# One-hot matrices made by three wide comparisons per group, with the weighing split between two engines

## The chip, the cores and the metric

The kernel runs on one core of a Trainium2 chip. The metric is device time in microseconds (us): the median of three runs of the kernel before is 2552.06 us (2551.03 to 2554.61). Where the text speaks of engines, PE is TensorE (matrix products; PEld are its weight loads), DVE is VectorE, ACT is ScalarE, POOL is GpSimd and SP is SyncE, which here only issues transfers.

## The reference

A graph of 3125 nodes and 103125 edges (both directions of 50000 random pairs, and a loop at each node, sorted by target) is used in two layers. The first makes ten hops of a normalised sum over neighbours, the second four steps of a gated unit whose messages depend on the edge's type.

```python
agg = jax.ops.segment_sum(feat[src] * e[:, None], dst, num_segments=N_NODES)   # first layer, 10 times
...
m = (embedding @ W_msg.T + b_msg).reshape(n, N_EDGE_TYPES, DIM)
q = m[src, etype]
r = jax.ops.segment_sum(q, dst, num_segments=n)                                # second layer, 4 times
embedding = _gru_cell(r, embedding, w_ih, w_hh, b_ih, b_hh)
```

Every sum over edges is a product with a matrix of counts: how many edges of each type go from node s to node t. The kernel builds this matrix once, on the chip, and uses it in all fourteen sums.

## The kernel before, in words

**Stages.** First the edges are loaded and turned into tables (`keys`, `tab`), 125 edges to a column, 825 columns. Then comes the counting stage, from 63.5 us to 534.1 us, in which all that the diff touches happens. After it come a check of the degrees, ten hops, and four steps of the gated unit.

**The counting stage.** The targets are cut into 125 groups of 25 nodes. The edges of one group lie in at most W = 8 columns of the tables (with a rare extra column, which an `If` on a loaded number handles). For a group q:

- POOL copies the eight columns' keys, weights and places into small buffers (`stage`, lines 361 to 366), and waits before that for the buffer to be free.
- DVE makes two one-hot matrices (`onehots`, lines 959 to 968). `hot_place` marks for each edge which of 128 places its source has: one comparison of 1024 elements. `hot_pair` marks for each edge which of 228 pairs (target within the group, source within its tile) it belongs to, multiplied by the edge's weight, a power of two that encodes its type: eight instructions of 228 elements, one a column.
- PE multiplies the two, column by column, eight products summed in one bank of PSUM (`count`, lines 599 to 612). Each product waits for its own `hot_pair` instruction (`s_hot`).
- ACT copies the sum from PSUM to `words` (`evacuate`, lines 457 to 461).

Eight groups are a block. After a block ACT cuts the three bytes (lanes) of its words apart (`part_lanes`, line 471, three instructions), SP stores them, and DVE sums the packed digits (`sum_digits`, lines 983 to 995, six instructions). All four engines run loops whose bodies are written out: on DVE 16 groups and two digit sums a turn, seven turns. The one-hot buffers are double, so POOL, DVE and PE are at most two groups apart.

Order on each engine is the order of the program; engines wait for each other by semaphores only. `wait_ge` stands in front of the instruction that follows it.

## Time and profile before

| | |
|---|---|
| median of three runs | 2552.06 us |
| profiled execution | 2550.86 us, its span 2549.3 us |
| counting stage (63.5 to 534.1 us) | 470.6 us of the span |
| PE busy | 2190.8 us, 86% |
| DVE busy | 1488.7 us, 58% |
| ACT busy | 335.0 us, 13% |
| POOL busy | 134.9 us, 5% |

The shares are means over stages with different limits. The rows below are of the counting stage, apart from one of the stage behind it that stands for a form of instruction.

### The profile page before, as it was taken

How to read it: one execution, taken by the hardware profiler on the slowest of the kernel's cores; microseconds unless marked ns; L12 is line 12 of the kernel's file. 1: busy time of each engine (PE TensorE's matmuls, PEld its weight loads, DVE VectorE, ACT ScalarE, POOL GpSimd, SP SyncE). 2: the span in 40 equal slices, each digit the busy share in tenths (PEclk: the TensorE clock that was granted, in tenths of full speed). 3: DMA queues.
4: the chain of work that ended last, by engine and by line, in shares of the span. 5: the costliest groups of instructions: out<-in, count | busy, mean ns of one | idle time of the engine just before them, and what ended most of it. 6: DMA issues, size and time to landing. Idle time of an engine off the chain costs nothing.

```text
span 2549.3 us, 41289 instructions
## 1 busy us (share of the span) xinstructions
PE 2190.8 (86%) x14375; PEld 1440.7 (57%) x14886; DVE 1488.7 (58%) x3473; ACT 335.0 (13%) x494; POOL 134.9 (5%) x391
## 2 busy tenths in 40 slices
PE   1544545559999999999799999999999999999996
PEld 1322333348999898988644455444554446544464
DVE  6988999977777777777662234522444324442243
ACT  0322223330000000000121011210112100220000
POOL 1322222200000000000000000000000000000000
PEclk9996555559999999999899999999999999999998
DMA  2000000010000000001400000000000000000001
GB/s 72 21 21 21 21 21 21 28 41 2 1 2 2 2 2 2 1 2 49 139 1 1 1 1 1 1 1 1 1 1 1 1 1 1 1 1 1 1 1 50
DMA packets 22188, 34.32 MB, mean 13 GB/s; under 512 B 2450, under 2 KB 18442, under 8 KB 21469
## 3 DMA queue, kind: packets, MB, share of 16 engines
q1 hardware_dynamic: 19025, 30.56, 3.5%
q8 instruction: 127, 2.08, 0.3%
q10 hardware_dynamic: 2944, 0.93, 0.2%
q14 instruction: 92, 0.75, 0.1%
HBM read 18.04 MB, written 13.45 MB: 12 GB/s over the span
## 4 chain that ended last, share of the span: by engine, by line
PE 75%; DVE 15%; issue 5%; DVEq 2%; DMA 2%; ACT 0%; POOLq 0%; ACTq 0%; POOL 0%
PE ps L787 41%; PE ps L706 26%; DVE hot_pair L967 8%; PE ps L739 3%; PE ps L727 2%; DVEq L961 2%; DVE dig L990 1%; DVE hot_place L964 1%; DVE big L993 1%; DMA big<-in_L_gnn_w_hh 1%; PE ps L647 1%; DMA x_after_hops<-x 1%; PE ps L691 1%; PE ps L605 1%; DVE dig L992 1%
## 5 line engine op out<-in xcount | busy, mean ns | idle before, releaser
L787 PE MATMUL ps<-slots,m_parts 125*128 125x500 fp8e4 (+1 forms) x5600 | 1088.0, 354 | 6.6 <-DVE m_parts L1337 5.2
L787 PEld LDWEIGHTS ps<-slots,m_parts 125*128 125x128 f16 x5600 | 547.4, 98 | 495.7 <-issue 10.0
L706 PE MATMUL ps<-parts,big 125*128 125x256 f16 x6125 | 669.6, 273 | 6.8 <-issue 4.2
L706 PEld LDWEIGHTS ps<-parts,big 125*128 125x128 fp8e4 x6125 | 591.3, 98 | 63.6
L605 PE MATMUL ps<-hot_pair,hot_place 125*128 125x228 f16 x1000 | 230.6, 400 | 256.5 <-DVE hot_pair L967 256.5
L1255 DVE TENSOR_SCALAR slots<-big 128x3200 int32<-128x3200 int32 (+1 forms) x112 | 244.1, 2183 | 279.8 <-PE ps L787 279.7
L605 PEld LDWEIGHTS ps<-hot_pair,hot_place 125*128 125x128 f16 x1000 | 143.1, 149 | 343.8 <-DVE hot_pair L967 283.1
L967 DVE TENSOR_SCALAR hot_pair<-iota_pair,win 125x228 f16<-125x228 f16 x1000 | 262.5, 334 | 3.1 <-issue 3.1
L1357 DVE SCALAR_TENSOR_TENSOR r_parts<-ps,over,r_parts 128x500 f16<-128x500 f32 (+1 forms) x28 | 19.1, 684 | 230.1 <-ACT r_parts L527 230.1
L1364 DVE SCALAR_TENSOR_TENSOR gate_r<-ps,over,gate_r 128x500 f32<-128x500 f32 (+1 forms) x28 | 19.1, 682 | 229.3 <-PE ps L739 221.8
L1183 DVE SCALAR_TENSOR_TENSOR hop_tmp<-ps,coef,g 125x128 f32<-125x128 f32 x250 | 87.6, 350 | 97.9 <-PE ps L706 94.4
L461 ACT ACTIVATE words<-ps 128x228 int32<-128x228 f32 x125 | 72.0, 602 | 354.4 <-PE ps L605 352.2
L964 DVE TENSOR_TENSOR hot_place<-iota_place,win_p 125x1024 f16<-125x1024 f16 x125 | 85.5, 684 | 48.2 <-issue 32.1
L727 PE MATMUL ps<-w_parts,emb_parts 128*125 128x512 f16 x300 | 84.7, 397 | 17.7 <-DVE m_full L1343 9.3
L527 ACT ACTIVATE r_parts<-ps,over 128x500 f16<-128x500 f32 (+1 forms) x28 | 17.7, 634 | 618.6 <-PE ps L787 618.6
L427 ACT ACTIVATE rs<-rs 125x25 f32<-125x25 f32 x3 | 0.7, 224 | 708.7 <-DVE rs L852 708.7
L1185 DVE SCALAR_TENSOR_TENSOR hop_tmp<-ps,coef,hop_tmp 125x128 f32<-125x128 f32 x250 | 87.8, 351 | 8.9
L1164 DVE TENSOR_SCALAR parts<-hop_tmp,scale 125x128 f16<-125x128 f32 x225 | 64.3, 286 | 36.4 <-DVE hop_tmp L1185 33.0
L1178 DVE SCALAR_TENSOR_TENSOR g<-hd,anchor,hop_tmp 125x128 f32<-125x128 f32 x225 | 79.0, 351 | 9.4 <-DVE hop_tmp L1177 0.7
L1167 DVE SCALAR_TENSOR_TENSOR parts<-hop_tmp,scale,parts 125x128 f16<-125x128 f32 x225 | 79.1, 352 | 8.0
L364 POOL TENSOR_TENSOR win<-keys,q_off 125x8 f32 (+1 forms) x125 | 65.3, 523 | 332.7 <-DVE hot_pair L967 318.5
L1343 DVE SCALAR_TENSOR_TENSOR m_full<-ps,bias_msg 125x512 f32<-125x512 f32 x100 | 68.3, 689 | 24.6 <-PE ps L727 23.6
(200 smaller groups left out, 1130.2 us busy)
## 6 DMA issues: line engine op xcount, KB each, us to landing
packed_counts<-packed SPq DMA_DIRECT2D x16, 625.0 KB, 3.3
big<-packed_counts SPq DMA_DIRECT2D x4, 1600.0 KB, 7.3
big<-packed_counts SPq DMA_DIRECT2D x3, 1200.0 KB, 6.5
hd<-in_x SPq DMA_DIRECT2D x1, 1562.5 KB
x_again<-in_x SPq DMA_DIRECT2D x1, 1562.5 KB
x_after_hops<-x SPq DMA_DIRECT2D x1, 1562.5 KB
big<-x_after_hops SPq DMA_DIRECT2D x1, 1562.5 KB
out<-big SPq DMA_DIRECT2D x4, 250.0 KB
```

The lines of the kernel that those rows point to most:

```text
L605: pe.matmul(ps[:, j, 0:KP], hot_place[0:CH, b, :, w], hot_pair[0:CH, b, w, :], start=w == 0, stop=w == W - 1, skip_group_check=True).then_ ...
L706: last = pe.matmul(ps[:, n % RING, 0:2 * F], tot_f8[0:Q, c, a, :], both((parts0, parts1)[par], a), start=a == 0, stop=a == TILES - 1)
L727: last = pe.matmul(ps[0:Q, 6 + a % 2, :], emb_parts[:, h, a, :], w_parts[:, w, :], start=n == 0, stop=n == 2)
L739: last = pe.matmul(out, g_parts[:, w, j * F:(j + 1) * F], value(h), start=start and m == 0, stop=stop and m == 2)
L787: last = pe.matmul(ps[:, k % 2, 0:SIZES[k] * Q], m_parts[0:Q, a, h, t * F:(t + 1) * F], slots_f8[0:Q, t % 2, 0:SIZES[k], a, 0:Q], start=a ...
L964: TT(hot_place[0:CH, b, :, :], iota_place[0:CH, :, :], win_p[0:CH, b:b + 1, :].broadcast_to([CH, 128, W]), ALU.is_equal)
L967: TS(hot_pair[0:CH, b, w, :], iota_pair[0:CH, :], win[0:CH, b, 0, w:w + 1], win[0:CH, b, 1, w:w + 1], ALU.is_equal, ALU.mult).then_inc(s_h ...
L1167: return STT(out=at[:, 1, :], in0=value, scalar=power, in1=at[:, 0, :], op0=ALU.mult, op1=ALU.subtract)
L1178: step(STT(out=tile_of(g, c), in0=tile_of(hd, c), scalar=anchor[0:Q, ds(h, 1)], in1=hop_tmp[0:Q, 2, :], op0=ALU.mult, op1=ALU.add))
L1183: step(STT(out=hop_tmp[0:Q, 0, :], in0=bank[:, 0:F], scalar=column(coef, c), in1=tile_of(g, c), op0=ALU.mult, op1=ALU.add))
L1185: step(STT(out=hop_tmp[0:Q, 1, :], in0=bank[:, F:2 * F], scalar=column(coef, c), in1=hop_tmp[0:Q, 0, :], op0=ALU.mult, op1=ALU.add))
L1255: TS(slots[:, t % 2, 0:n * 4].bitcast(I32).rearrange("p (n b w) -> p n b w", b=NB, w=2), big1[:, first:first + n * 4].bitcast(I32).rearran ...
```

## The change

For each group DVE now issues three instructions in place of nine. `marks` compares all eight columns with 128 places in one instruction (1024 elements, laid out column by column and no longer interleaved). `hot_pair` compares all eight columns with the 228 pairs in one instruction (1824 elements), without the weight. The weight now goes into the other factor, `weighed = marks * weight`: for the first WA = 5 columns ACT does this, one instruction of 128 elements a column with the weight as a scale, and for the last WD = 3 columns DVE does it in one instruction (384 elements). In the comparisons the small operand is read through a pattern whose innermost run is two elements: POOL writes each key, place and weight twice, side by side, and the pattern reads that pair 64 or 114 times before it goes on to the next column.

Around that: buffers are four deep (DEPTH) and no longer two; POOL does four small instructions a group and no longer three; PE waits once for the pairs, five times for ACT's columns and once for DVE's; ACT's `evacuate` of a group comes after the weighing of the group two later, and the three lanes of a block are cut apart one at a time, after the fourth, fifth and sixth group of the next block; `sum_digits` has five instructions and no longer six, and stands after the seventh group of the next block; the loops of DVE and ACT have 32 groups written out (three turns), that of PE 16. Key spacing KQ goes from 1024 to 456, and the differences are now held in 16 bits; a path for inputs that need larger counts is adapted and doesn't run with these inputs.

```diff
+DEPTH = 4
+ROUND = 4
+WA = 5
+WD = W - WA
...
+            def stage_window(q, b):
+                lo = pool.value_load(windows[0:1, ds(q, 1)], min_val=0, max_val=NCH)
+                pool.wait_ge(s_hot_used, q + 1)
...
+                pool.tensor_copy(win_place[0:CH, b, :, :], twice(tab[0:CH, 0, ds(lo, W)]))
+                pool.tensor_copy(win_f[0:CH, b, :, :], twice(tab[0:CH, 1, ds(lo, W)]))
+                pool.tensor_copy(win_w[0:CH, b, :], tab[0:CH, 1, ds(lo, W)])
+                pool.tensor_tensor(win_key[0:CH, b, :, :], twice(keys[0:CH, ds(lo, W)]),
+                                   q_off[0:CH, ds(q, 1)].rearrange("p (w o) -> p w o", o=1).broadcast_to([CH, W, 2]),
+                                   ALU.subtract).then_inc(s_wst, 1)
...
+            def weigh(q, b):
+                act.wait_ge(s_marks, q + 1)
+                for w in range(WA):
+                    act.activation(weighed[0:CH, b, w, :], marks[0:CH, b, w, :], ACT.Copy,
+                                   scale=win_w[0:CH, b, w:w + 1]).then_inc(s_weighed, 1)
+
+            def block_of(turn, b, n, turn_before):
                 blk = 2 * turn + b
-                act.wait_ge(s_bytes, blk + 1)
                 for j in range(n):
-                    evacuate(blk, b, j)
-                part_lanes(blk, turn, b, BQ * blk + n - 1)
...
+                    weigh(BQ * blk + j, j % DEPTH)
+                    if j >= 2:
+                        evacuate(blk, b, j - 2)
+                    elif turn_before is not None:
+                        evacuate(2 * turn_before + 1 - b, 1 - b, BQ - 2 + j)
+                    if 3 <= j < 3 + LANES and turn_before is not None:
+                        part_lane(turn_before, 1 - b, j - 3, 16 * turn_before + BQ * (1 - b) + BQ - 1)
...
                 pe.wait_ge(s_taken, q + 1)
+                pe.wait_ge(s_pairs, q + 1)
                 for w in range(W):
-                    pe.wait_ge(s_hot, W * q + w + 2 * W + 1)
-                    pe.matmul(ps[:, j, 0:KP], hot_place[0:CH, b, :, w], hot_pair[0:CH, b, w, :],
-                              start=w == 0, stop=w == W - 1, skip_group_check=True).then_inc(s_hot_used, 1)
+                    if w < WA:
+                        pe.wait_ge(s_weighed, WA * q + w + 1)
+                    elif w == WA:
+                        pe.wait_ge(s_weighed_d, q + 1)
+                    last = pe.matmul(ps[:, j, 0:KP], weighed[0:CH, b, w, :], hot_pair[0:CH, b, w, :],
+                                     start=w == 0, stop=w == W - 1, skip_group_check=True)
+                last.then_inc(s_hot_used, 1)
...
-                dve.wait_ge(s_hot_used, W * q + W)
-                TT(hot_place[0:CH, b, :, :], iota_place[0:CH, :, :],
-                   win_p[0:CH, b:b + 1, :].broadcast_to([CH, 128, W]), ALU.is_equal)
-                for w in range(W):
-                    TS(hot_pair[0:CH, b, w, :], iota_pair[0:CH, :], win[0:CH, b, 0, w:w + 1],
-                       win[0:CH, b, 1, w:w + 1], ALU.is_equal, ALU.mult).then_inc(s_hot, 1)
+                dve.wait_ge(s_hot_used, q + 1)
...
+                def row(m, count, n):
+                    return m.rearrange("p (o n two) -> p o n two", o=1, two=2).broadcast_to([CH, count, n // 2, 2])
+
+                def each(m, count, n):
+                    return m.rearrange("p w (o two) -> p w o two", o=1).broadcast_to([CH, count, n // 2, 2])
+
+                TT(by_two(marks[0:CH, b, :, :], 128), row(iota_row[0:CH, :], W, 128),
+                   each(win_place[0:CH, b, :, :], W, 128), ALU.is_equal).then_inc(s_marks, 1)
+                TT(by_two(hot_pair[0:CH, b, :, :], KP), row(iota_pair[0:CH, :], W, KP),
+                   each(win_key[0:CH, b, :, :], W, KP), ALU.is_equal).then_inc(s_pairs, 1)
+                dve.wait_ge(s_marks, q + 1)
+                TT(by_two(weighed[0:CH, b, WA:W, :], 128), by_two(marks[0:CH, b, WA:W, :], 128),
+                   each(win_f[0:CH, b, WA:W, :], WD, 128), ALU.mult).then_inc(s_weighed_d, 1)
...
-                TS(high, low, NIBBLES, None, ALU.bitwise_and)
-                step(TS(lower, low, 4, NIBBLES, ALU.logical_shift_right, ALU.bitwise_and))
-                step(TT(big1[:, :].bitcast(DT.uint16).rearrange("p (n q) -> p n q", q=64)[:, :, ds(4 * blk, 4)],
-                        u16[1].rearrange("p (n q) -> p n q", q=4), u16[2].rearrange("p (n q) -> p n q", q=4), ALU.add))
+                step(TT(low16, low16, high16, ALU.add))
+                step(TS(high16, low16, 1.0 + 1.0 / 16, None, ALU.mult))
+                step(TS(big1[:, :].bitcast(I32).rearrange("p (n q) -> p n q", q=32)[:, :, ds(2 * blk, 2)],
+                        high.rearrange("p (n q) -> p n q", q=2), NIBBLES, None, ALU.bitwise_and))
...
+                for j in range(BQ):
+                    onehots(BQ * (blk + 1) + j, j % DEPTH)
+                    if j == BQ - 2:
+                        sum_digits(blk, b)
+
+            with dve.Fori(0, (NB - 2) // ROUND) as i:
+                steps.loop(i, 4 * ROUND)
+                for k in range(ROUND):
+                    block_of(ROUND * i + k, k % 2)
...
             sum_digits(NB - 2, 0)
-            for q in range(BQ * (NB - 1) + HEAD, Q):
-                onehots(q, q % 2)
```

On DVE, one group inside the loop stood so in the program before (the register work in front loads the group's number of extra columns; the branch behind leaves out the extra columns):

```order
L961 ISA
L961 TENSOR_LOAD windows_row
L961 ISA x2
L962 REGISTER_ALU
L963 ISA
L964 TENSOR_TENSOR hot_place<-iota_place,win_p 125x1024
L967 TENSOR_SCALAR hot_pair<-iota_pair,win 125x228 x8
L969 COMPARE_AND_BRANCH
```

It stands so in the changed program:

```order
L1025 ISA
L1025 TENSOR_LOAD windows_row
L1025 ISA x2
L1026 REGISTER_ALU
L1038 TENSOR_TENSOR marks<-iota_row,win_place 125x1024
L1040 TENSOR_TENSOR hot_pair<-iota_pair,win_key 125x1824
L1043 TENSOR_TENSOR weighed<-marks,win_f 125x384
L1045 COMPARE_AND_BRANCH
```

Nine engine instructions between the same register work have become three; the third (L1043) carries the wait for the first.

On ACT, the end of a block of eight groups stood so before: the last copy out of PSUM, the three lanes, then the next copy's register work.

```order
L461 ACTIVATE words<-ps 128x228
L464 REGISTER_ALU
L466 ISA
L471 ACTIVATE packed<-words 128x1800 x2
L471 ACTIVATE packed<-words 128x1400
L476 REGISTER_ALU
L459 ISA
```

In the changed program the fifth group of a block stands so, with one lane of the block before behind it:

```order
L516 ACTIVATE weighed<-marks,win_w 125x128 x5
L494 REGISTER_ALU
L489 ISA
L489 TENSOR_LOAD windows_row
L489 ISA x3
L498 ACTIVATE words<-ps 128x228
L509 ACTIVATE packed<-words 128x1800
```

Each group has gained five instructions on ACT, and the lanes have been moved from behind a block to between the weighings of the next one.

## Rows read from the trace of the kernel before

**Rows 1.** Windows: stretch, its length, busy time (count) by engine, PE clock, DMA

```profile
63.50:521.20 457.70, 230.45 (x1000) 143.05 (x1000) 418.30 (x1220) 138.47 (x169) 128.07 (x372) 0.67 0.06 22
...
102.19:162.19 60.00, 29.57 (x128) 18.32 (x128) 53.93 (x157) 18.15 (x22) 17.17 (x48) 1.00 0.06 22
...
222.15:281.97 59.82, 29.50 (x128) 18.30 (x128) 53.92 (x156) 18.15 (x22) 17.15 (x48) 0.50 0.06 22
```

**Rows 2.** Waits from 100 to 680 us: who for whom, total, times, longest

```profile
POOL win L364 <- DVE hot_pair L967: 296.4, 111, 10.8
ACT words L461 <- PE ps L605: 295.0, 84, 12.7
...
PE ps L605 <- DVE hot_pair L967: 216.3, 119, 10.6
...
DVE hot_place L964 <- issue: 32.1, 14, 4.1
```

**Rows 3.** Timeline of DVE, the first group: start, length, instruction

```profile
63.52 0.69 DVE L964 TENSOR_TENSOR hot_place<-iota_place,win_p 125x1024 f16<-125x1024 f16 x1 [15.20 <-POOL win_p L366]
64.13 2.09 DVE L967 TENSOR_SCALAR hot_pair<-iota_pair,win 125x228 f16<-125x228 f16 x8
66.14 0.68 DVE L964 TENSOR_TENSOR hot_place<-iota_place,win_p 125x1024 f16<-125x1024 f16 x1
```

**Rows 4.** Timeline of DVE: one digit sum, restarts after two of them

```profile
94.96 0.80 DVE L988 TENSOR_SCALAR dig<-packed 128x1250 int32<-128x1250 int32 x1
...
96.51 1.46 DVE L990 TENSOR_TENSOR dig<-dig 128x2500 uint16<-128x2500 uint16 x1
98.01 0.81 DVE L991 TENSOR_SCALAR dig<-dig 128x1250 int32<-128x1250 int32 x1
...
99.69 1.46 DVE L993 TENSOR_TENSOR big<-dig 128x2500 uint16 x1
102.19 0.69 DVE L964 TENSOR_TENSOR hot_place<-iota_place,win_p 125x1024 f16<-125x1024 f16 x1 [1.03 <-issue]
...
133.46 0.69 DVE L964 TENSOR_TENSOR hot_place<-iota_place,win_p 125x1024 f16<-125x1024 f16 x1 [4.13 <-issue]
...
134.85 1.84 DVE L967 TENSOR_SCALAR hot_pair<-iota_pair,win 125x228 f16<-125x228 f16 x7 [0.45 <-issue]
```

**Rows 5.** Groups by line and form, 100 to 680 us: busy, mean ns, idle before

```profile
L964 DVE TENSOR_TENSOR hot_place<-iota_place,win_p 125x1024 f16<-125x1024 f16 x113 | 77.3, 684 | 33.0 <-issue 32.1 <-DVE big L993 0.8
...
L990 DVE TENSOR_TENSOR dig<-dig 128x2500 uint16<-128x2500 uint16 x15 | 22.0, 1468 | 0.5
...
L1267 DVE TENSOR_TENSOR hd<-hd,to_hd 125x3200 f32<-125x3200 f32 x1 | 3.5, 3492 | 0.0
```

**Rows 6.** Timeline of ACT: three lanes, two copies out, 25 instructions with a scale

```profile
114.55 4.57 ACT L471 ACTIVATE packed<-words 128x1800 uint8<-128x1800 uint8 x3
119.02 1.01 ACT L461 ACTIVATE words<-ps 128x228 int32<-128x228 f32 x2
...
555.94 7.40 ACT L507 ACTIVATE parts<-hd,to_hd 125x128 f16<-125x128 f32 x25 [1.80 <-DVEq L1160]
```

**Rows 7.** Timeline of POOL beside DVE's instructions

```profile
110.36 0.41 POOL L364 TENSOR_TENSOR win<-keys,q_off 125x8 f32 x1 [1.82 <-DVE hot_pair L967]
...
124.78 1.42 POOL L366 COPY win_p<-tab 125x8 f16 x1
```

**Rows 8.** Timeline of PE: the eight products of two groups

```profile
106.14 1.82 PE L605 MATMUL ps<-hot_pair,hot_place 125*128 125x228 f16 x8 [0.79 <-DVE hot_pair L967]
108.80 1.78 PE L605 MATMUL ps<-hot_pair,hot_place 125*128 125x228 f16 x8 [0.83 <-DVE hot_pair L967]
```

**Rows 9.** Timeline of DVE: the end of the counting stage

```profile
521.13 4.92 DVE L1046 BATCH_NORM_STATS2 stat_x<-hd 125x6 f32<-125x128 f32 x25
...
528.05 0.81 DVE L988 TENSOR_SCALAR dig<-packed 128x1250 int32<-128x1250 int32 x1
...
532.67 1.46 DVE L993 TENSOR_TENSOR big<-dig 128x2500 uint16<-128x2500 uint16 x1
```

More of the change, by code:

```diff
@@ L51 @@
 KP = 228
-KQ = 1024
+KQ = 456
+KG = 1024
+NOWHERE = -4096.0
 BQ = 8
@@ L196, in build @@
             packed = sb("packed", [128, 2, BLOCK_BYTES], U8, b)
-            dig = sb("dig", [128, 3, BLOCK_BYTES // 4], I32, b)
+            dig = sb("dig", [128, 2, BLOCK_BYTES // 4], I32, b)
+            hot_pair = sb("hot_pair", [128, DEPTH, W, KP], F16, b)
+            marks = sb("marks", [128, DEPTH, W, 128], F16, b)
+            weighed = sb("weighed", [128, DEPTH, W, 128], F16, b)
         with ExitStack() as b:
@@ L366, in stage, with twice @@
                 pool.tensor_copy(win_p[0:CH, b, :], tab[0:CH, 0, ds(lo, W)]).then_inc(staged, 1)
-            with pool.Fori(0, Q // 2) as i:
-                stage(2 * i, 2 * i, 0, s_hot, s_wst)
-                stage(2 * i + 1, 2 * i + 1, 1, s_hot, s_wst)
-            stage(Q - 1, Q - 1, 0, s_hot, s_wst)
+            def stage_window(q, b):
+                lo = pool.value_load(windows[0:1, ds(q, 1)], min_val=0, max_val=NCH)
+                pool.wait_ge(s_hot_used, q + 1)
+                def twice(m):
+                    return m.rearrange("p (w o) -> p w o", o=1).broadcast_to([CH, W, 2])
+                pool.tensor_copy(win_place[0:CH, b, :, :], twice(tab[0:CH, 0, ds(lo, W)]))
[4 more added lines that the diff above has]
+                                   ALU.subtract).then_inc(s_wst, 1)
+            with pool.Fori(0, Q // DEPTH) as i:
+                for j in range(DEPTH):
+                    stage_window(DEPTH * i + j, j)
+            for q in range(Q // DEPTH * DEPTH, Q):
+                stage_window(q, q % DEPTH)
             def share_largest():
@@ L458, in evacuate @@
                 q = BQ * blk + j
[L459 removed]
+                act.wait_ge(s_hot_used, q + 1 + DEPTH)
                 summed(q, extras, s_more_used)
+                if j == 0:
+                    act.wait_ge(s_bytes, blk + 1)
                 act.activation(words[:, b, :, j], ps[:, j, 0:KP], ACT.Copy, scale=float(ONE)).then_inc(s_taken, 1)
[L463 to L472 removed]
@@ L474, in block_of, with part_lane @@
-            def block_of(turn, b, n):
+            def part_lane(turn, b, l, last):
+                blk = 2 * turn + b
+                if l == 0:
+                    act.wait_ge(s_taken, last + 1 + BANKS)
+                    act.wait_ge(s_digits, blk + 1)
+                    act.wait_ge(s_packed[b], 16 * turn + 16)
+                lanes = words[:, b, :, :].bitcast(U8).rearrange("p n (q l) -> p (n q) l", l=4)
+                n = min(LANE, TILES - l * LANE) * TILES * BQ
+                at = l * LANE * TILES * BQ
+                ins = act.activation(packed[:, b, at:at + n], lanes[:, 0:n, l], ACT.Copy)
+                if l == LANES - 1:
+                    ins.then_inc(s_bytes, 1)
@@ new lines, in block_of @@
+                    if 3 <= j < 3 + LANES and turn_before is not None:
+                        part_lane(turn_before, 1 - b, j - 3, 16 * turn_before + BQ * (1 - b) + BQ - 1)
+            block_of(0, 0, BQ, None)
+            with act.Fori(0, (NB - 2) // ROUND) as i:
+                for k in range(ROUND // 2):
+                    turn = ROUND // 2 * i + k
+                    block_of(turn, 1, BQ, turn)
+                    block_of(turn + 1, 0, BQ, turn)
+            for turn in range((NB - 2) // ROUND * ROUND // 2, NB // 2 - 1):
+                block_of(turn, 1, BQ, turn)
+                block_of(turn + 1, 0, BQ, turn)
@@ L486, in _ @@
+            block_of(NB // 2 - 1, 1, Q - (NB - 1) * BQ, NB // 2 - 1)
+            evacuate(NB - 1, 1, 3)
+            part_lane(NB // 2 - 1, 0, 2, BQ * (NB - 1) - 1)
+            evacuate(NB - 1, 1, 4)
+            for l in range(LANES):
+                part_lane(NB // 2 - 1, 1, l, Q - 1)
             root(1)
@@ L636, in count_general @@
                                   start=False, stop=False, skip_group_check=True).then_inc(s_more_used_g, 1)
-            with pe.Fori(0, NB - 1) as i:
-                for j in range(BQ):
-                    count(BQ * i + j, j % 2, j)
-            for j in range(Q - (NB - 1) * BQ):
-                count(BQ * (NB - 1) + j, j % 2, j)
+            PER_TURN = BQ * ROUND // 2
+            with pe.Fori(0, Q // PER_TURN) as i:
+                for j in range(PER_TURN):
+                    count(PER_TURN * i + j, j % DEPTH, j % BANKS)
+            for q in range(Q // PER_TURN * PER_TURN, Q):
+                count(q, q % DEPTH, q % BANKS)
             pe.wait_ge(s_digits, NB + 2)
```

70 lines of the change are left out of this document (33 added, 37 removed).

## The prediction, written before the changed kernel had run

> **What bounds the kernel now.** I read the windows first. The counting stage runs from 63.5 to 521.2 us with DVE busy for 418.3 of 457.7 us, PE for half of it, ACT and POOL for under a third each [rows 1]. Two windows of two blocks, one at a PE clock of 1.00 and one at 0.50, are 60.00 and 59.82 us long: PE's clock doesn't matter here. The waits say the same from the other side: POOL, ACT and PE all wait in the end for DVE's `hot_pair`, DVE itself only for "issue", time in which nothing that the profile shows held it [rows 2]. So the stage is a single chain of DVE instructions. Its parts, from the timeline:
>
> - a group: 66.14 − 63.52 = 2.62 us, of which `hot_place` takes 0.61 until the next may start and the eight `hot_pair` 2.01 [rows 3];
> - a digit sum: from 94.96 to 99.69 + 1.46 = 101.15, so 6.19 us [rows 4];
> - a restart after it: 1.03 us of "issue" (DVE has run dry, and reads the group's number before it can start) [rows 4];
> - a backward jump of the loop: the stall is 4.13 us and not 1.03, with 0.45 more behind the first instruction [rows 4]. Of the 32.1 us of such idle time in 14 pieces [rows 2], 8 are plain: (32.1 − 8 × 1.03) / 6 = 3.98, so a jump costs 3.98 + 0.45 − 1.03 = 3.4 us; seven turns have six jumps;
> - at the end, statistics of x between 521.13 and 528.05, then the last digit sum until 534.13 [rows 9].
>
> 125 × 2.62 + 16 × 6.19 + 14 × 1.03 + 6 × 3.4 + 6.9 = 468.3 us, where 534.13 − 63.52 = 470.6 are measured; 2.3 us stay unexplained, and I keep them. Everything behind the stage is untouched.
>
> **The change, part by part.**
>
> *DVE's group.* Two forms with two 16-bit inputs are in the trace: 1024 elements in 684 ns and 2500 in 1468 ns [rows 5], so 0.531 ns per element and 0.14 us fixed, and the next instruction starts about 0.08 us before the end of one [rows 3]. `marks` (1024) then costs 0.605 until the next may start, `hot_pair` (1824: 1.109 long) 1.03, the third (384: 0.344 long) 0.27. Sum 1.905 us. The third waits for the first, which ended some 0.9 us earlier: nothing. But only three instructions are queued now, and behind the third come the branch and the register work that takes 1.03 us when DVE has run dry [rows 4]. It can begin when `marks` is through, 0.7 us into the group, so the next group starts at 1.8 to 2.0 us and not surely at 1.905. I take 1.97, and 1.905 and 2.1 as bounds. 125 × 1.97 = 246.3 us.
>
> *Whether the small operand streams.* This is the largest unknown: the run of two elements is one 4-byte word, read again and again. The full-rate row reads runs of eight 16-bit elements. One row reads a single word 128 times over: L1267 multiplies hd by a factor per tile through a step of zero, 3200 elements in 3492 ns [rows 5], 1.04 ns each beyond 0.16 fixed, as fast as 32-bit data go elsewhere in DVE's two-input work. Re-reading one word costs nothing there, so I take 0.531 ns. The bounds are 0.531 and 1.04 ns per element (pairs not taken together at all).
>
> The Trainium skill ("Vector Engine (DVE) Microarchitecture Reference", 5.1) says that two elements per partition do run in the two-at-once mode. Its section 5.2 speaks against the change: a port streams at full rate only in runs of at least two adjacent 4-byte words, and one source that hops at every word takes 1.73 ns in place of 1.054. By that ratio a group would cost 1.10 us more. Whether reading one word again counts as a hop isn't said, and L1267's row speaks against it.
>
> *Digit sum.* Its last two instructions are one-input now: 0.81 us each by L991's row (1250 32-bit words) [rows 4], if the 2500 16-bit elements are taken as fast as their bytes. 1.55 + 1.50 + 0.85 + 0.81 = 4.71 us; at one element a cycle for one of them it is about 0.65 more (bound: + 10 us in all). 16 × 4.71 = 75.4, and 14 restarts again 14.4.
>
> *Jumps.* Three turns have two: 2 × 3.4 = 6.8 us, 13.6 less than before.
>
> *ACT.* An instruction of 128 elements with a scale per partition costs (7.40 − 0.39) / 24 = 0.292 us in a row of 25 [rows 6]. A copy out of PSUM costs 1.01 − 0.60 = 0.41 behind another, three lanes 119.02 − 114.55 = 4.47 [rows 6]. A group is 5 × 0.292 + 0.41 = 1.87, just under DVE's; a block is 8 × 1.87 + 4.47 = 19.4 us. On average it fits, but not where the lanes stand. They follow groups 3, 4 and 5 of a block, and DVE's digit sum follows group 6 and needs them. From the start of group 3 ACT is through at 0.74 + 3 × 1.87 + 4.47 = 10.8 us; DVE is there after 4 × 1.97 = 7.9. DVE waits 2.9 us in each of 14 blocks: **a new wait, 41 us**. At the end the lanes of block 14 are through 0.74 + 2 × 1.46 + 3 × 0.41 + 4.47 = 9.4 us after group 123 starts, DVE after 3.9: 5.4 us. Buffers four deep keep ACT's lag (up to 3.4 us) from DVE.
>
> *POOL.* Its reads get through only between two of DVE's long instructions: a copy that takes 0.2 us otherwise took 1.42 beside a digit instruction, and the subtraction 0.41 beside `hot_place` [rows 7]. With three instructions of DVE and four of POOL per group POOL falls short by one slot a group, but gains at the digit sum and in the waits; staging runs four groups ahead. I take 4 us, bounds 0 and 30.
>
> *PE.* Eight products take 1.78 us, then 0.83 idle, part of it PE's own branch [rows 8]: at most 2.61 us a group, 20.9 us a block. That is below a block's length in the sum below, so PE is late within a block but not over it: nothing.
>
> **Sum.** 246.3 + 75.4 + 14.4 + 6.8 + 6.9 + 41 + 5.4 + 4 + 2.3 = 402.5 us, in place of 470.6: 68 us less. Against the profiled execution of 2550.9 that is 2483. The median of the runs shown is 1.2 us above it: I predict **2485 us**. A block would be 8 × 1.97 + 4.71 + 1.03 + 2.9 = 24.4 us, where it was 29.9.
>
> **The rivals.**
>
> - *ACT doesn't overlap its weighings* (each carries its own semaphore): 0.387 us in place of 0.292, a group 2.35, a block at least 8 × 2.35 + 4.47 = 23.3, and ACT idles for 4.1 us between its lanes and the first marks after the digit sum. A block is 27.4 us, 3.0 more: 14 × 3.0 = 42, so 2527 us. For it: the marks and scales come fresh from other engines. Against: the 25 of [rows 6] signal too.
> - *POOL's four instructions set the pace* (each waits for an end on DVE, 0.6 us a piece): 2.4 us a group in a run of eight, partly in place of the wait for the lanes. 8 × 2.4 + 5.7 = 24.9, and 1 to 2 us for the lanes: 26.5, so 2.1 × 14 = 29 more: 2515 us.
> - *The run of two is slow: slower than before.* The place is the three comparisons' 3232 elements per group. With 1.04 ns each the group is 1.97 + 3232 × 0.51 ns = 3.6 us; ACT's waits vanish: 125 × 3.6 + 75.4 + 14.4 + 6.8 + 6.9 + 2.3 = 556, so 2638 us. The change pays until the group is (470.6 − 105.8) / 125 = 2.92 us, that is, up to 0.82 ns per element.
> - *The page's hop rule*, as a mechanism of this kernel: pairs are taken together, but each new run of the small operand costs part of a cycle. Half-way between the two rows, 0.79 ns, it gives a group of 2.8 us and 455 us of stage: 2537 us. The ratio of the Trainium skill's section 5.2 would give a group of 3.07 and about 2571, estimated from that page.
> - *The change gives more*: ACT's lanes wait for less, or register work is hidden throughout (−8 us): 2465.
>
> **How the numbers follow.** Forecast with its own range 2462 to 2505: 0.58. ACT without overlap 0.12, POOL 0.12, the hop rule 0.07 (in half of it slower than before), slow runs of two 0.09, something not thought of 0.02. From 2462 to 2540 about 0.83 of it lies. A measurement of this kernel tells 0.2%, 5 us, from no change. Faster 0.85, same 0.02, slower 0.13.
>
> **What would show it.** In the changed profile: `marks` near 0.68 us, `hot_pair` near 1.11, the third near 0.34 (else the third or fourth rival); a wait of DVE's first digit instruction for ACT's lanes, 14 or 15 times some 3 us; ACT busy for over 80% of the stage; stalls of 4 us twice and not six times; starts of `marks` 1.9 to 2.0 us apart. ACT's five weighings start 0.29 us apart (else the first rival); `marks` waiting for POOL at nearly every group would be the second. The prediction is wrong if a group of DVE exceeds 2.2 us, or if the sequence of waits between the four engines locks step in a way that the sum, which takes each engine's wait singly, doesn't see.

## The result, and the profile after

| | before | after |
|---|---|---|
| median | 2553.34 us (4 runs, 2551.03 to 2561.13) | 2482.55 us (4 runs, 2481.51 to 2484.49) |
| ratio of the times | | 0.9718, 95% interval 0.9696 to 0.974 |
| profiled execution | 2550.86 us, span 2549.3 | 2481.51 us, span 2480.0 |
| counting stage | 63.52 to 534.13: 470.6 us | 64.45 to 473.11: 408.7 us |
| from the stage's end to the end of the span | 2015.2 us | 2006.9 us |

The kernel is 2.8% faster, and the predicted 2485 us is 2.5 us off. But two errors cancel in it: the stage was forecast at 402.5 us and took 408.7, and behind the stage, where I had put nothing, 8.3 us went. How much of the 8.3 is scatter between executions is asked further down.

The page of the kernel after first: lines of its part 1 and its costliest groups, to lay beside [rows 5] and the table of before.

```profile
PE 2164.4 (87%) x14375; PEld 1409.1 (57%) x14886; DVE 1392.8 (56%) x2707; ACT 502.2 (20%) x1119; POOL 236.5 (10%) x517
...
L516 ACT ACTIVATE weighed<-marks,win_w 125x128 f16<-125x128 f16 x625 | 195.5, 389 | 121.0 <-DVE marks L1038 119.9
...
L1040 DVE TENSOR_TENSOR hot_pair<-iota_pair,win_key 125x1824 f16<-125x1824 f16 x125 | 137.5, 1100 | 0.0
L1038 DVE TENSOR_TENSOR marks<-iota_row,win_place 125x1024 f16<-125x1024 f16 x125 | 86.0, 688 | 43.7 <-POOL win_key L395 24.3
```

`marks` takes 688 ns and `hot_pair` 1100, as forecast (0.68 and 1.11 us); (1100 − 688) / 800 = 0.52 ns an element, where 0.53 was taken. So the small operand, read in runs of two, holds nothing up, and the third and fourth rival are out. Re-reading one 4-byte word is no hop of the kind that the Trainium skill's "Vector Engine (DVE) Microarchitecture Reference", section 5.2, prices; the measured rows decide. Its ratio would have given 2571 us, by the estimate in the prediction.

Where POOL and DVE wait in the stage, from the list of waits (who waits for whom: us in all, times, longest):

```profile
POOL win_place L392 <- PE ps L668: 151.7, 48, 6.3
DVE dig L1064 <- ACT packed L509: 43.0, 15, 5.5
DVE marks L1038 <- POOL win_key L395: 24.3, 8, 16.1
DVE marks L1038 <- DVE big L1068: 9.9, 10, 1.0
```

The first line is POOL waiting for a free buffer, which costs nothing. The second is the new wait, forecast as 14 times 2.9 and once 5.4, 46.4 us in all. Of the third, 16.1 us are the wait before the stage begins. DVE's timeline at the first digit sum, then at the first backward jump (start us, us; in brackets the idle time before):

```profile
94.51 1.10 DVE L1040 TENSOR_TENSOR hot_pair<-iota_pair,win_key 125x1824 f16<-125x1824 f16 x1
95.54 0.35 DVE L1043 TENSOR_TENSOR weighed<-marks,win_f 125x384 f16<-125x384 f16 x1
98.44 0.81 DVE L1064 TENSOR_SCALAR dig<-packed 128x1250 int32<-128x1250 int32 x1 [2.56 <-ACT packed L509]
99.17 0.81 DVE L1065 TENSOR_SCALAR dig<-packed 128x1250 int32<-128x1250 int32 x1
100.01 1.46 DVE L1066 TENSOR_TENSOR dig<-dig 128x2500 uint16<-128x2500 uint16 x1
101.50 0.82 DVE L1067 TENSOR_SCALAR dig<-dig 128x2500 uint16<-128x2500 uint16 x1
102.47 1.46 DVE L1068 TENSOR_SCALAR big<-dig 128x1250 int32 x1
...
180.62 0.69 DVE L1038 TENSOR_TENSOR marks<-iota_row,win_place 125x1024 f16<-125x1024 f16 x1 [1.01 <-DVE big L1068]
...
185.46 0.69 DVE L1038 TENSOR_TENSOR marks<-iota_row,win_place 125x1024 f16<-125x1024 f16 x1 [2.86 <-POOL win_key L395]
```

A digit sum takes 102.47 + 1.46 − 98.44 = 5.49 us and not 4.71: its last instruction takes 1.46 us where 0.81 was forecast, and starts 102.47 − 101.50 = 0.97 us after the one before it where 0.85 was. The stall at the jump (185.46 − 180.62 = 4.84 between two starts, where a group takes 1.90) appears twice: 5.9 us in all, forecast 6.8.

ACT's timeline at the same place. Five weighings take 1.55 us in a row, (1.55 − 0.39) / 4 = 0.29 apart, so ACT overlaps them and the first rival is out. The third lane ends at 98.40, and DVE's digit sum starts at 98.44:

```profile
91.81 1.55 ACT L516 ACTIVATE weighed<-marks,win_w 125x128 f16<-125x128 f16 x5
93.26 0.56 ACT L498 ACTIVATE words<-ps 128x228 int32<-128x228 f32 x1
93.62 1.71 ACT L509 ACTIVATE packed<-words 128x1800 uint8<-128x1800 uint8 x1
95.23 1.55 ACT L516 ACTIVATE weighed<-marks,win_w 125x128 f16<-125x128 f16 x5
96.68 0.56 ACT L498 ACTIVATE words<-ps 128x228 int32<-128x228 f32 x1
97.03 1.37 ACT L509 ACTIVATE packed<-words 128x1400 uint8<-128x1400 uint8 x1
```

Last, POOL and DVE early in the stage, from the timelines of both:

```profile
66.59 0.70 POOL L393 COPY win_f<-tab 125x16 f16 x1
67.24 1.06 POOL L394 CAST win_w<-tab 125x8 f32 x1
68.27 0.33 POOL L395 TENSOR_TENSOR win_key<-keys,q_off 125x16 f16 x1
...
66.54 0.69 DVE L1038 TENSOR_TENSOR marks<-iota_row,win_place 125x1024 f16<-125x1024 f16 x1
67.15 1.10 DVE L1040 TENSOR_TENSOR hot_pair<-iota_pair,win_key 125x1824 f16<-125x1824 f16 x1
68.17 0.35 DVE L1043 TENSOR_TENSOR weighed<-marks,win_f 125x384 f16<-125x384 f16 x1
68.63 0.69 DVE L1038 TENSOR_TENSOR marks<-iota_row,win_place 125x1024 f16<-125x1024 f16 x1
```

POOL's `win_f` copy ends with DVE's `marks` (67.29 and 67.23), its cast with `hot_pair` (68.30 and 68.25), and `win_key` at 68.60, 0.03 us before the next `marks` may start. So the group is 2.09 us long and not 1.90. Call the time from one `marks` to the next a pitch. Of 49 pitches between 2.05 and 2.6 us, 38 are of this kind (`marks` starts within 0.15 us of the end of its `win_key`; five of them are over 2.2 us).

Two of the forecast's signs came out off the mark: ACT was busy for 317.3 of 408.7 us, 78% and not over 80%, and of the 110 pitches without a digit sum only 58 were shorter than 2.05 us.

### The profile page after: what moved, and what is told of

It reads as the page before. It is cut to its first block, busy times and chain, and to the rows that moved or that the text cites. A ratio compares the mean times of both kernels' runs of the same rounds, so it can differ in the third digit from the quotient of the medians.

```text
span 2480.0 us, 40786 instructions
## 1 busy us (share of the span) xinstructions
PE 2164.4 (87%) x14375; PEld 1409.1 (57%) x14886; DVE 1392.8 (56%) x2707; ACT 502.2 (20%) x1119; POOL 236.5 (10%) x517
## 4 chain that ended last, share of the span: by engine, by line
PE 77%; DVE 8%; ACT 6%; issue 4%; DMA 2%; ACTq 1%; DVEq 1%; POOL 1%; POOLq 0%
PE ps L852 42%; PE ps L771 26%; PE ps L804 3%; ACT weighed L516 3%; PE ps L792 2%; ACT packed L509 2%; ACT words L498 1%; ACTq L489 1%; DVE marks L1038 1%; DVE dig L1066 1%; DVE big L1068 1%; DMA big<-in_L_gnn_w_hh 1%; DMA x_after_hops<-x 1%; PE ps L712 1%; PE ps L668 1%
## 5 line engine op out<-in xcount | busy, mean ns | idle before, releaser
L771 PE MATMUL ps<-parts,big 125*128 125x256 f16 x6125 | 669.6, 273 | 6.2 <-DVEq L1385 4.0
L771 PEld LDWEIGHTS ps<-parts,big 125*128 125x128 fp8e4 x6125 | 591.2, 98 | 63.5
L668 PE MATMUL ps<-hot_pair,weighed 125*128 125x228 f16 x1000 | 209.9, 358 | 207.6 <-ACT weighed L516 121.7
L668 PEld LDWEIGHTS ps<-hot_pair,weighed 125*128 125x128 f16 x1000 | 113.4, 120 | 303.9 <-ACT weighed L516 266.3
L516 ACT ACTIVATE weighed<-marks,win_w 125x128 f16<-125x128 f16 x625 | 195.5, 389 | 121.0 <-DVE marks L1038 119.9
L1040 DVE TENSOR_TENSOR hot_pair<-iota_pair,win_key 125x1824 f16<-125x1824 f16 x125 | 137.5, 1100 | 0.0
L1038 DVE TENSOR_TENSOR marks<-iota_row,win_place 125x1024 f16<-125x1024 f16 x125 | 86.0, 688 | 43.7 <-POOL win_key L395 24.3
L792 PE MATMUL ps<-w_parts,emb_parts 128*125 128x512 f16 x300 | 83.4, 393 | 19.3 <-DVE m_full L1426 10.8
L394 POOL CAST win_w<-tab 125x8 f32 x125 | 85.3, 683 | 0.0
L578 ACT ACTIVATE m_parts<-m_full 125x512 f16<-125x512 f32 x100 | 62.6, 630 | 88.6 <-DVE m_full L1426 88.5
```

Of the source, the lines that this page charges most:

```text
L394: pool.tensor_copy(win_w[0:CH, b, :], tab[0:CH, 1, ds(lo, W)])
L516: act.activation(weighed[0:CH, b, w, :], marks[0:CH, b, w, :], ACT.Copy, scale=win_w[0:CH, b, w:w + 1]).then_inc(s_weighed, 1)
L668: last = pe.matmul(ps[:, j, 0:KP], weighed[0:CH, b, w, :], hot_pair[0:CH, b, w, :], start=w == 0, stop=w == W - 1, skip_group_check=True)
L771: last = pe.matmul(ps[:, n % RING, 0:2 * F], tot_f8[0:Q, c, a, :], both((parts0, parts1)[par], a), start=a == 0, stop=a == TILES - 1)
L792: last = pe.matmul(ps[0:Q, 6 + a % 2, :], emb_parts[:, h, a, :], w_parts[:, w, :], start=n == 0, stop=n == 2)
L1038: TT(by_two(marks[0:CH, b, :, :], 128), row(iota_row[0:CH, :], W, 128), each(win_place[0:CH, b, :, :], W, 128), ALU.is_equal).then_inc(s_m ...
```

## The experiments

Twelve kernels ran. "Stage" is from the first `marks` (or `hot_place`) to the end of the last digit sum. "Hops" is from the start of the first product of PE's loop over the hops (L771 in the kernel after, 6125 of the 6250 products) to that of the last, "gated steps" the same for all products with the messages. Each is from the timeline of the profiled execution.

| kernel | us (median) | ratio to before, 95% | stage | hops | gated steps |
|---|---|---|---|---|---|
| before | 2553.34 | | 470.6 | 675.6 | 1250.6 |
| after | 2482.55 | 0.9696 to 0.974 | 408.7 | 675.0 | 1241.4 |
| e1_digit16 | 2483.74 | 0.9706 to 0.9738 | 408.9 | 675.2 | 1242.2 |
| e2_round2 | 2501.05 | 0.978 to 0.9817 | 427.1 | 675.0 | 1241.1 |
| e3_lanes | 2441.24 | 0.9546 to 0.9581 | 366.7 | 674.9 | 1241.4 |
| e4_runs_of_one | 2642.19 (one run) | | 567.4 | 675.1 | 1240.9 |
| e5_merge | 2436.20 | 0.9528 to 0.956 | 363.0 | 675.6 | 1241.6 |
| e6_wa0 | 2474.02 | 0.9670 to 0.9702 | 399.0 | 678.8 | 1241.5 |
| e7_contig | 2472.90 (one run) | | 398.5 | 676.7 | 1241.4 |
| e8_shift | 2555.35 | 0.9991 to 1.0012 | 471.0 | 677.2 | 1249.4 |
| e9_loads32 | 2547.38 | 0.9956 to 0.998 | 471.1 | 678.7 | 1241.1 |
| e10_wa6 | 2444.53 | 0.9553 to 0.9582 | 369.9 | 674.8 | 1241.3 |
| e11_round14 | 2432.78 | 0.9506 to 0.9532 | 352.2 | 679.9 | 1243.8 |
| e12_pe_as_was | 2423.43 | 0.9482 to 0.9508 | 349.5 | 675.2 | 1241.2 |

**e4_runs_of_one: is the run of two what pays?** The small operand's pattern (`each`) repeats one element; the other operands of the three comparisons are read without pairs, here shown for `marks`.

```diff
-    return m.rearrange("p w (o two) -> p w o two", o=1).broadcast_to([CH, count, n // 2, 2])
+    return m[:, :, 0:1].broadcast_to([CH, count, n])
...
-TT(by_two(marks[0:CH, b, :, :], 128), row(iota_row[0:CH, :], W, 128),
+TT(marks[0:CH, b, :, :], row1(iota_row[0:CH, :], W, 128),
```

> The three comparisons read their small operand as a plain broadcast of one element (step zero, runs of one), not as runs of two. Theory A: the run of two is what lets 16-bit elements be taken two at a time; runs of one take 1.04 ns an element: 3232 x 0.51 = 1.65 us a group more, the wait for ACT's lanes (43 us) goes: 125 x 1.65 - 43 = 163 us more, 2645 us; marks 1.2 us, hot_pair 2.05. Rival B: re-reading a word costs nothing either way, the run of two isn't needed: marks 0.69, hot_pair 1.10, 2482 us.

Its costliest groups on DVE in the stage, from the lines of the trace:

```profile
L1043 DVE TENSOR_TENSOR hot_pair<-iota_pair,win_key 125x1824 f16<-125x1824 f16 x113 | 231.5, 2049 | 0.0
L1041 DVE TENSOR_TENSOR marks<-iota_row,win_place 125x1024 f16<-125x1024 f16 x113 | 137.6, 1218 | 34.4 <-POOL win_key L395 15.9 <-DVE big L1071 10.1 <-PE ps L668 3.6
```

Theory A, to 3 us. The pattern with runs of one takes (2049 − 1100) / 1824 = 0.52 ns an element more, and the wide comparison then loses to the kernel before. All that the change gains hangs on each small value being read in runs of two, for which it is written twice.

**e3_lanes: the wait for ACT's lanes.**

```diff
-if 3 <= j < 3 + LANES and turn_before is not None:
-    part_lane(turn_before, 1 - b, j - 3, 16 * turn_before + BQ * (1 - b) + BQ - 1)
+if 1 <= j < 1 + LANES and turn_before is not None:
+    part_lane(turn_before, 1 - b, j - 1, 16 * turn_before + BQ * (1 - b) + BQ - 1)
...
-part_lane(NB // 2 - 1, 0, 2, BQ * (NB - 1) - 1)
```

> ACT cuts the three lanes after groups 1, 2 and 3 of the next block instead of 3, 4 and 5, two groups of some 2 us earlier. Theory A: DVE's wait for the lanes (43 us in 15 pieces) is only a matter of that order and goes: 14 x 2.7 + 5 = 43 us less, 2440 us. ACT lags behind DVE by 1.4 us more at each of three groups, 4 us in all, which buffers four deep take. Rival B: the wait comes back as DVE's wait for a free buffer (ACT and PE late at groups 4 to 6), half the gain: 2461 us. Rival C: POOL, starved by DVE's back-to-back instructions, then sets the pace (marks waits for win_key at most groups, pitch 2.5 us): 8 x 0.45 x 14 = 50 us come back, no gain: 2482 us or more.

Theory A, to 1 us: 41 us less than after. From its list of waits:

```profile
DVE marks L1037 <- POOL win_key L395: 28.8, 12, 16.2
DVE marks L1037 <- PE ps L667: 9.4, 10, 1.0
DVE dig L1063 <- ACT packed L509: 3.3, 1, 3.3
```

Of 43.0 us 3.3 are left, at the end of the stage, and neither POOL nor the free buffers took the place of the rest (the 9.4 us for PE are ten restarts behind digit sums, which the kernel after pays as well). The wait was a matter of the order in ACT's program.

**e1_digit16 and e7_contig: the digit sum's last instruction.** The first takes the same bytes as 16-bit elements. The second writes them side by side, in an order that the rest of the kernel doesn't expect; it serves only to time the instruction.

```diff
-step(TS(big1[:, :].bitcast(I32).rearrange("p (n q) -> p n q", q=32)[:, :, ds(2 * blk, 2)],
-        high.rearrange("p (n q) -> p n q", q=2), NIBBLES, None, ALU.bitwise_and))
e1:
+step(TS(big1[:, :].bitcast(DT.uint16).rearrange("p (n q) -> p n q", q=64)[:, :, ds(4 * blk, 4)],
+        high16.rearrange("p (n q) -> p n q", q=4), NIBBLES & 0xffff, None, ALU.bitwise_and))
e7:
+step(TS(big1[:, :].bitcast(I32)[:, ds(BLOCK_BYTES // 4 * blk, BLOCK_BYTES // 4)],
+        high, NIBBLES, None, ALU.bitwise_and))
```

> The last instruction of the digit sum works on 2500 16-bit elements with output runs of four, instead of 1250 32-bit words with output runs of two. Theory A: its 1.46 us came from 32-bit words taken one a cycle when the output lies in runs of two, and 16-bit elements are taken as fast as the multiplication just before it (2500 in 0.82 us): 16 x 0.64 = 10 us less, all on DVE's path, 2472 us. Rival B: scattered output is what is slow, whatever the type, one element a cycle: 2500 x 1.04 = 2.6 us, 16 x 1.15 = 18 us more, 2501 us. Rival C: the bytes set the time, 1.46 us as now, 2482 us.

> The changed kernel with the last digit instruction writing its 1250 words side by side and not in 625 runs of two; the digits of a block then lie in another order than the rest of the kernel expects, so the output isn't the reference's. Theory A: the scattered output makes it 1.46 us; side by side it takes 0.81: 16 x 0.65 = 10 us less, 2472 us. Rival B: the operation (a bit operation on words this late in a chain, or its input) sets 1.46: 2482 us.

The instruction's row in e1, then in e7, from the lines of each trace:

```profile
L1068 DVE TENSOR_SCALAR big<-dig 128x2500 uint16 x12 | 17.5, 1456 | 1.7
```

```profile
L1068 DVE TENSOR_SCALAR big<-dig 128x1250 int32 x12 | 9.8, 813 | 1.7
```

e1: rival C, 1456 ns for twice the elements. e7: theory A, 813 ns, and the stage is 408.7 − 398.5 = 10.2 us shorter. So the way in which the output lies costs this instruction 0.64 us, whatever the type of the elements.

Runs of 8 bytes alone need not be the reason, though. The output goes to 625 of them, an odd number. Both kernels have another instruction with one input that works in runs of two words, that of `unpack` in the gated steps (it reads them so), over 100 or 75 rows of 16 runs. From the lines of the kernel before:

```profile
L1255 DVE TENSOR_SCALAR slots<-big 128x2400 int32<-128x2400 int32 x48 | 127.9, 2665 | 97.0 <-PE ps L787 97.0
L1255 DVE TENSOR_SCALAR slots<-big 128x3200 int32<-128x3200 int32 x64 | 116.2, 1822 | 182.8 <-PE ps L787 182.8
```

With 100 rows it takes 1822 / 3200 = 0.57 ns a word, with 75 rows 2665 / 2400 = 1.11: the smaller one is the slower. That makes the odd count a rival. No run writes the digits in an even number of runs, so which of the two it is stays open.

**e2_round2: the backward jumps.**

```diff
-ROUND = 4
+ROUND = 2
```

> Loops written out over 16 groups again (8 on PE), everything else as in the changed kernel. Theory A: DVE jumps back six times and not twice, each jump costs the 3 us beyond a restart that the changed kernel's trace shows: 4 x 3 = 12 us more, 2494 us. Rival B: the jump overlaps the wait for ACT's lanes, which is 2.9 us a block anyway: 2484 us. On the 8 us that the changed kernel gained behind the counting stage: if the placement of code in memory is the cause, the four gated steps (1241.4 us there, 1250.6 before) change by some us although nothing in them is touched; if it isn't, they stay at 1241 +- 1.

Measured: 18.5 us more, where A said 12. The jumps show as "issue" in its list of waits:

```profile
DVE marks L1038 <- issue: 24.5, 9, 3.7
```

Six pitches are 5.70 us and not 1.90, 3.8 a jump, where the longer loop paid 2.9 (4.84): 22.8 − 5.9 = 16.9 us. POOL adds to it, with 52 pitches of its kind and not 38. The mechanism is A's, the price of a jump was taken from the wrong loop. The wait for the lanes stayed (41.2 us), so rival B is out. The gated steps stayed at 1241.1 us although PE's code ahead of them had got shorter. By the test that I had set, that speaks against code placement as the cause of the gain there; e9 below speaks for it.

**e5_merge: POOL's instructions.**

```diff
-pool.tensor_copy(win_place[0:CH, b, :, :], twice(tab[0:CH, 0, ds(lo, W)]))
-pool.tensor_copy(win_f[0:CH, b, :, :], twice(tab[0:CH, 1, ds(lo, W)]))
+pool.tensor_copy(win_two[0:CH, b, :, :, :], tab[0:CH, :, ds(lo, W)]
+                 .rearrange("p j (w o) -> p j w o", o=1).broadcast_to([CH, 2, W, 2]))
```

> On top of e3_lanes. POOL copies places and weights of a group in one instruction of 32 elements instead of two of 16, so three instructions a group and not four. In the trace of e3_lanes 40 of 110 groups have a pitch of 2.09 us and not 1.90, and there marks starts 0.04 us after POOL's win_key ends. Theory A: POOL's instructions get through only between two of DVE's, one a slot, and with four instructions POOL falls short by one slot; with three it keeps ahead: 43 x 0.19 + 4 x 0.6 = 11 us less, 2430 us, nearly all pitches 1.90. Rival B: the delay is a cost per element read, the merged copy takes as long as the two: 2441 us. Rival C: the 0.19 us is DVE held up at the port by POOL's reads and not a wait; fewer instructions halve it at best: 2437 us.

5 us less (3.7 in the stage), half of A's and the time that rival C gave. The pitches say why: of those between 2.05 and 2.6 us in e3_lanes, 33 of 45 had `marks` start within 0.15 us of the end of `win_key`; here 2 of 20. The mechanism is A's, a wait: C has DVE's instructions held up at the port, but `marks` and `hot_pair` take 0.69 and 1.10 us beside POOL's as elsewhere. The gain is small because POOL was not the only cause. The other 18 slow pitches recur at the same places of each turn of the loop, with `win_key` ready long before. In each of them DVE's register work behind the branch starts 0.3 us late (at 1.21 to 1.32 us into the group and not at 0.93). Eight of the 33 pitches in e3_lanes have this delay too: 25 were POOL's alone, and 9 of the 38 in the kernel after are of both kinds. In e12_pe_as_was, without a loop, one slow pitch is left. Why the register work starts late at these places isn't in the trace.

**e6_wa0 and e10_wa6: the split of the weighing.** On e3_lanes `WA = 0`, on e5_merge `WA = 6`.

> On top of e3_lanes. WA = 0: DVE weighs all eight columns itself (1024 elements in place of 384), ACT none. Theory A: DVE is the bound, so this costs 0.335 us a group, 42 us, less the 11 us of waits for POOL, whose lock at 2.09 us is below the new pitch of 2.24: 2472 us. Rival B: ACT's share hides another delay (products start later, since all eight wait for DVE's third instruction; buffers come free later): more than 2485 us. Rival C: DVE wasn't the bound in e3_lanes, ACT and POOL were: 2450 us or less.

> On top of e5_merge, WA = 6: ACT weighs six columns, DVE two (256 elements instead of 384). Theory A: DVE is the bound throughout, its third instruction gets shorter by 128 x 0.53 = 0.07 us: 8.5 us less, 2428 us. ACT has 8 x (6 x 0.292 + 0.41) + 4.47 = 21.8 us of work a block, DVE 8 x 1.95 + 5.45 + 1.03 = 22.1 us. Rival B: ACT, now as loaded as DVE, comes late with the columns and with the free buffers (four deep), and DVE waits for PE: 2436 us or up to 2450.

e6: 2474.0, theory A by the total, so ACT's share is worth 33 us against e3_lanes. One step of A is wrong, though: POOL's lock did not fall below the new pitch, it moved with it (24 pitches of 2.42 us instead of 2.24). From the timelines of e6, POOL and DVE:

```profile
73.32 1.06 POOL L394 CAST win_w<-tab 125x8 f32 x1
74.34 0.66 POOL L395 TENSOR_TENSOR win_key<-keys,q_off 125x16 f16 x1
...
73.22 1.10 DVE L1039 TENSOR_TENSOR hot_pair<-iota_pair,win_key 125x1824 f16<-125x1824 f16 x1
74.25 0.68 DVE L1042 TENSOR_TENSOR weighed<-marks,win_f 125x1024 f16<-125x1024 f16 x1
75.04 0.69 DVE L1037 TENSOR_TENSOR marks<-iota_row,win_place 125x1024 f16<-125x1024 f16 x1
```

`win_key` ends at 75.00, behind DVE's third instruction (74.93), and `marks` starts at 75.04. In such groups one of POOL's instructions gets through for each of DVE's, whatever its length. The Trainium skill ("SBUF — State Buffer", "SBUF: two separate sides") says that DVE with two inputs and GpSimd share a pair of ports, which one of them holds for a whole instruction. The trace agrees: in the kernel after the cast takes 0.19 us where DVE is idle (at 112.73) and 1.06 beside `hot_pair`. One for one is not a law: four times in the kernel after, a copy of 0.2 us into `win_place` took 3.88 us, from 108.77 to 112.65 the first time, while DVE ran six instructions without a pause, and ended as DVE fell idle.

e10: rival B, 8.3 us slower than e5. The mean of the pitches below 2.05 us fell by 0.045 us, but from its list of waits:

```profile
DVE dig L1062 <- ACT packed L508: 15.2, 14, 4.9
```

ACT has become nearly as long as DVE, and the wait for the lanes is back. Of none, five and six columns, five is best.

**e8_shift and e9_loads32: where did 8.3 us behind the stage come from?** In the kernel before PE stalls at the start of the second, third and fourth gated step. PE's weight loads at the second step's start, from the timeline:

```profile
1587.53 0.41 PEld L727 LDWEIGHTS ps<-w_parts,emb_parts 128*125 128x125 f16 x3 [3.14 <-DVE m_full L1343]
1588.02 0.10 PEld L570 LDWEIGHTS <-ones 128*128 128x128 f16 x1
1588.06 0.10 PEld L787 LDWEIGHTS ps<-slots,m_parts 125*128 125x128 f16 x1
1590.04 0.10 PEld L787 LDWEIGHTS ps<-slots,m_parts 125*128 125x128 f16 x1 [1.88 <-issue]
```

and the windows of the same place (length; busy time of PE, PEld, DVE, ACT and POOL; then the granted clock, DMA share and GB/s):

```profile
1588.00:1590.00 2.00, 0.40 (x2) 0.14 (x2) 1.65 (x4) 1.28 (x2) 0.00 (x0) 0.69 0.00 0
1590.00:1594.00 4.00, 3.97 (x10) 1.72 (x11) 2.11 (x5) 1.25 (x3) 0.00 (x0) 0.50 0.00 0
```

The weight loads in the kernel after:

```profile
1529.64 0.41 PEld L792 LDWEIGHTS ps<-w_parts,emb_parts 128*125 128x125 f16 x3 [3.06 <-DVE m_full L1426]
1530.12 0.10 PEld L629 LDWEIGHTS <-ones 128*128 128x128 f16 x1
1530.16 0.70 PEld L852 LDWEIGHTS ps<-slots,m_parts 125*128 125x128 f16 x4
```

Before: one weight load, then 1.88 us of "issue", nothing that the profile shows; after this pause and the one before it the granted clock is 0.50 (1.2 GHz) in the 4 us that follow. After: no stall, and a clock of 1.00. The code is the same; only what stands ahead of it in PE's program differs. The first of the two experiments adds 64 register moves there, the second 32 weight loads.

```diff
 for j in range(Q - (NB - 1) * BQ):
     count(BQ * (NB - 1) + j, j % 2, j)
+for k in range(64):
+    pe.reg_mov(extras, 0)                                          # e8
+for k in range(32):
+    pe.ldweights(ones16[:, :], tile_position=(0, 0))               # e9
```

> The kernel before, with 64 register moves more in PE's program behind the counting loop and nothing else. They are issued once and cost below 4 us at a place where PE waits for DVE's last digit sum, so nothing by themselves. Theory A: the 8 us that the changed kernel gained behind the counting stage come from where PE's code lies in memory: the four gated steps take 1241 us and not 1250.6, 2544 us. Rival B: something else of the kernel before keeps them at 1250: 2553 us.

> The 64 register moves of e8_shift left no trace: the instruction count is that of the kernel before (41289), the moves were folded away, so that run only repeated the kernel before and its gated steps (1249.4 us). Here PE issues 32 real weight loads behind the counting loop, some 3 us where it waits for DVE anyway. Theory A: the placement of PE's code decides whether PE stalls for 1.9 us at the start of each gated step (between the first weight load of L787 and its product) and then runs for 5 us at half clock: the four steps change by at least 3 us from 1250, down to 1241, and the kernel takes about 2545 us. Rival B: it isn't PE's code, the steps stay at 1250 +- 1.5 us, 2553 us.

e8 tests nothing: the moves aren't in the compiled program, which has 41289 instructions, as many as the kernel before. So it is the same program once more. It shows that the 1250 us are no accident of one profile (1249.4 here), and how much two executions can differ: 677.2 us in the hops in place of 675.6, and 2019.3 us behind the stage in place of 2015.2. In e9 the page's row of these loads falls from "issue 10.0" to 1.7; first before's row, then e9's:

```profile
L787 PEld LDWEIGHTS ps<-slots,m_parts 125*128 125x128 f16 x5600 | 547.4, 98 | 495.7 <-issue 10.0
```

```profile
L789 PEld LDWEIGHTS ps<-slots,m_parts 125*128 125x128 f16 x5600 | 547.0, 98 | 488.4 <-issue 1.7
```

Theory A: 32 more instructions make the kernel before 7.7 us faster (ratio 0.9968, interval 0.9956 to 0.998), with 9.5 us off the gated steps. In the hops it takes 3 us more than the kernel before, half of which is within what e8 differs by. At the second step's start its four weight loads of L789 come without a stall; a shorter stretch at half pace is still there (loads 0.42 us apart from 1594.90 to 1597.43). The Trainium skill ("Runtime: NRT & Kernel Launch", "Instruction fetch mechanics") says that a taken branch to code that isn't at hand waits for a fetch. The trace agrees in part: the branch of this loop (L782) takes 3.3 to 3.8 us at each of its three jumps in the kernel before, but 3.3 to 3.6 in the kernel after too, and the stall of 1.88 us begins 1.1 us behind its end. The fetch itself isn't in the trace, so that it is the cause stays likely and not shown. Apart from e8 and e11, every other kernel here spends 1240.9 to 1242.2 us in the gated steps, with PE's code ahead of them of several lengths, so it is the kernel before that is the exception.

**e11_round14 and e12_pe_as_was: no loops, and the best version.** On e5_merge `ROUND = 14`; in e12 PE keeps its loop of 16 groups (`PER_TURN = BQ * 2`).

> On top of e5_merge, the whole counting stage written out (DVE 14 blocks, ACT 7 pairs of blocks, PE 56 groups a turn). Theory A: DVE's two backward jumps, 2.9 us each beyond a restart, go: 6 us less, 2430 us. Rival B: written-out code is fetched for the first time all along and runs no faster than the loop did, or stalls at places of its own: 2436 us or more.

> e11_round14 with PE's counting loop as in the changed kernel (16 groups a turn) and only DVE and ACT written out. In e11_round14 the counting stage got 11 us shorter than in e5_merge, but the hops took 4.3 us and the gated steps 2.2 us longer. Theory A: that is PE's longer code, which moves the later loops in memory as the 32 loads of e9_loads32 did; with PE's code as in e5_merge the hops take 675.6 and the gated steps 1241.6 us again, and the stage keeps its 11 us: 2426 us. Rival B: PE's own backward jumps delay the products and DVE waits for free buffers, which e11_round14 had avoided: 2433 us or more. Rival C: the hops and steps were longer for another reason (other engines' code), and stay so: 2433 us.

e11: the stage is 10.8 us shorter (A had 6: the restarts also fall from 1.01 to 0.83 us, and the late pitches go), but the hops take 4.3 and the gated steps 2.2 us more, and only 3.4 us arrive. e12: theory A, hops and steps are back, the stage is 13.5 us shorter than in e5 (A had 11), 2423.4 us. DVE's wait for ACT's lanes and for POOL in e12, from the list of waits (15.7 us are the start of the stage):

```profile
DVE marks L1036 <- POOL win_key L394: 16.5, 2, 15.7
DVE dig L1062 <- ACT packed L508: 3.4, 1, 3.4
```

## Why the prediction was right, and where it was not

Step by step, with the stage's 408.7 us:

- *DVE's group*: forecast 1.97 us from 1.905 of instructions and partly exposed register work, 246.3 us, and 4 for POOL. Measured about 249 us, but by other parts: 1.90 where nothing disturbs (238 us), 7 us more in 29 groups that waited for POOL alone, and 4 in 20 groups whose register work started late, 9 of which waited for POOL as well. The size was right, the reason half right. The second rival ("POOL sets the pace") is true in 29 to 38 of 124 pitches, mostly at 2.09 and not 2.4 us.
- *The run of two streams*: right (1100 ns), and e4 shows that it decides all.
- *The new wait*: 43.0 us, forecast 46.4. e3 shows its cause.
- *Digit sum*: **the mis-sized term.** I took one-input instructions at the rate of the contiguous row; 4.71 × 16 = 75.4 us were 87.2. Of the 11.8 us, 10.2 are the way in which the last instruction's output lies (e7), the rest mostly its later start. I had named 10 us as the bound, which is what this one instruction cost; the whole error went beyond it.
- *Jumps* 5.9 (forecast 6.8), *restarts* 14.2 (14.4), *statistics* 7.1 (6.9), *ACT's overlap* 0.29 us: right. *PE* hardly ever held DVE up (0.3 us once). Of the 2.3 us kept as unexplained, 1.3 are the extra column of one group, a pitch of 3.22 us.
- *"Everything behind the stage is untouched"*: **the step that failed.** Untouched code ran 8.3 us faster, 9.2 of them less in the gated steps and 0.9 more elsewhere. That it comes from where the code lies is what e9 speaks for; e2 moved the code too and changed nothing there. That this made up for most of the digit sum's 11.8 us is luck: without it the kernel would have taken about 2491 us, still inside the range.

What the change is worth by its own means is the stage's 61.9 us. Of its parts the loops written out twice as long are worth 18 us (e2), the split of the weighing 33 us (e6, with the lanes moved), and the order that it brought cost 41 us (e3). These overlap and don't add up to the 61.9.

## What to carry to other kernels

Where an engine gets new work, walk through its program in order to the place that another engine waits for: the average load fitted here, and yet 41 us were lost to three instructions that stood two groups late. A small operand read again and again with 16-bit data should be stored twice and read in runs of two; here that took the instruction from 2049 to 1100 ns (e4). And a gain of a few us behind the edited place may have nothing to do with the edit: measure the same kernel with some idle instructions ahead of that place before you claim or mourn it, and count the instructions of the compiled program to see that they are in it.
